# The spiking network's first product as one float32 product, without high and low halves

## What is computed

```
x = x + layernorm(L0_ffn(layernorm(x)))
# L0_ffn(x, W_fc, W_proj):
h = square(relu(einsum('bsd,fd->bsf', x, W_fc)))     # 128 -> 512: the first product
y = einsum('bsf,df->bsd', h, W_proj)                 # 512 -> 128
# five steps; spikes are counted:
reset = spike(mem - 1); mem = 0.9 * mem + y - reset; spk = spike(mem - 1)
return sum(spks) / 5
```

## Time and profile before

| | us |
|---|---|
| median of 3 runs | 934.92 |
| lowest, highest | 934.91, 935.84 |
| profiled execution, its own time | 935.99 |
| its span (first to last instruction) | 934.1 |
| TensorE busy | 818.9 (88%) |
| VectorE busy | 682.9 (73%) |
| ScalarE busy | 586.2 (63%) |
| GpSimd busy | 430.6 (46%) |
| TensorE granted clock, mean | 0.954 of 2.4 GHz |

### The profile page before, as it was taken

The page is one execution under the profiler, slowest core; times in us unless marked ns, Lnnn a source line. Parts: engine busy times, 40 slices in busy tenths (PEclk is TensorE's granted clock), DMA queues, the critical chain, the costliest instruction groups (busy, mean ns, idle before and its releaser), DMA issues. The chain is left out here.

```text
span 934.1 us, 15863 instructions
## 1 busy us (share of the span) xinstructions
PE 818.9 (88%) x5364; PEld 713.6 (76%) x5364; DVE 682.9 (73%) x1919; ACT 586.2 (63%) x1244; POOL 430.6 (46%) x737
## 2 busy tenths in 40 slices
PE   0789889999999999999999999998959888877664
PEld 0688778888888888888888888987748676765553
DVE  4667878887888888878888878676448876677741
ACT  2545657777777777777777777675665456443343
POOL 6653424544454445444544454334444433344333
PEclk9969989999999999999999999999979899999986
DMA  9100000000001000100010000000000000000001
GB/s 292 27 1 2 1 1 1 13 23 1 1 2 35 1 1 2 35 1 2 1 35 2 1 1 1 2 1 1 2 1 1 1 1 1 12 12 12 11 12 34
DMA packets 19726, 13.68 MB, mean 15 GB/s; under 512 B 2487, under 2 KB 18494, under 8 KB 19646
## 3 DMA queue, kind: packets, MB, share of 16 engines
q1 hardware_dynamic: 18924, 12.47, 4.6%
q10 hardware_dynamic: 722, 0.20, 0.1%
HBM read 10.57 MB, written 2.10 MB: 14 GB/s over the span
## 5 line engine op out<-in xcount | busy, mean ns | idle before, releaser
L311 PE MATMUL PS<-W,HL 128*128 128x128 f32 x1536 | 202.6, 276 | 0.0
L311 PEld LDWEIGHTS PS<-W,HL 128*128 128x128 f32 x1536 | 194.2, 192 | 8.1
L696 POOL TENSOR_TENSOR JOIN<-STATS 128x8 f32<-128x8 f32 (+1 forms) x58 | 15.5, 267 | 238.0 <-DVE STATS L1136 238.0
L873 ACT ACTIVATE HL<-PS 128x512 f32<-128x512 f32 x192 | 109.3, 594 | 19.3 <-PE PS L311 15.0
L943 ACT ACTIVATE EK<-PS,NKM 128x512 f32<-128x512 f32 x48 | 33.0, 688 | 99.6 <-DVE NKM L1246 99.6
L311 PE MATMUL PS<-X2H,W1L 128*128 128x512 f32 x192 | 88.9, 463 | 6.1 <-issue 3.8
L859 ACT ACTIVATE XR<-XI,RSTD 128x128 f32<-128x128 f32 x224 | 71.7, 396 | 33.2 <-POOL RSTD L713 30.0
L1136 DVE BATCH_NORM_STATS2 STATS<-XI 128x6 f32<-128x128 f32 x416 | 89.4, 278 | 1.8 <-POOL JOIN L697 1.5
L752 POOL TENSOR_TENSOR QB<-QB,QRC 128x512 f32<-128x512 f32 x48 | 50.9, 1060 | 81.0 <-DVE QRC L1277 81.0
L321 PE MATMUL PS<-ID,XR 128*128 128x128 f32 x416 | 65.6, 281 | 21.8 <-ACT XR L859 21.7
L321 PEld LDWEIGHTS PS<-ID,XR 128*128 128x128 f32 x416 | 48.7, 143 | 37.9 <-issue 18.8
(11 more groups left out here) (207 smaller groups left out, 2133.4 us busy)
## 6 DMA issues: line engine op xcount, KB each, us to landing
W<-in_w SPq DMA_DIRECT2D x12, 256.0 KB
X<-in_x SPq DMA_DIRECT2D x8, 256.0 KB, 5.0
out<-X SPq DMA_DIRECT2D x8, 256.0 KB, 2.3
QKV<-in_qkv SPq DMA_DIRECT2D x6, 192.0 KB, 3.3
FWD<-in_fwd SPq DMA_DIRECT2D x1, 1024.0 KB, 6.1
INV<-in_inv SPq DMA_DIRECT2D x1, 1024.0 KB, 8.8
WO<-in_wo SPq DMA_DIRECT2D x6, 64.0 KB
FWDX<-in_fwdx SPq DMA_DIRECT2D x1, 256.0 KB, 6.4
```

What stands on the lines that cost most here:

```text
L311: return nc.tensor.matmul(o, l, r, start=start, stop=stop, skip_group_check=True)
L873: nc.scalar.activation(HL[f][:, :], pH[f % 2][:, :], ACT.Prelu, alpha=LEAK).then_inc(s["hl"], 1)
```

## The change

The spiking network's first product becomes one float32 product, FCC x X2F, in place of three. ScalarE writes twice the centred weights once, as float32 (FCC), and signals fc_out itself; VectorE's FCL goes. ScalarE copies the transposed input of items 48 to 55 into X2F (float32) and not into X2H; X2L is made for items 0 to 47 alone. h 0, state_turn and shift_turn wait for ScalarE's copy (x2h) where they waited for X2L. ScalarE's copy gets two waits, since X2F is now read by TensorE and, for the last item of the layers, by VectorE.

```
-        FCH, FCL = sb("FCH", [FB * P], F32R), sb("FCL", [FB * P], F32R)
+        FCC = sb("FCC", [FB * P])
...
                 if f == 0:
                     if item < ITEMS:
                         pe.wait_ge(s["w1_lo"], item // BATCH + 1)
+                        pe.wait_ge(s["x2l"], item + 1)
                     else:
                         pe.wait_ge(s["fc_out"], 1)
-                    pe.wait_ge(s["x2l"], item + 1)
+                        pe.wait_ge(s["x2h"], item + 1)
...
-                high, low = (W1H[w], W1L[w]) if item < ITEMS else (FCH, FCL)
                 o = slice(f * P, (f + 1) * P)
-                split3(pH[f % 2][:, :], high[:, o], low[:, o], X2H[:, :], X2L[:, :]).then_inc(s["h_ps"], 1)
+                if item < ITEMS:
+                    last = split3(pH[f % 2][:, :], W1H[w][:, o], W1L[w][:, o], X2H[:, :], X2L[:, :])
+                else:
+                    last = mm(pH[f % 2][:, :], FCC[:, o], X2F[:, :])
+                last.then_inc(s["h_ps"], 1)
...
             def state_turn(v, n):
                 pe.wait_ge(s["st_x"], v + 1)
-                pe.wait_ge(s["x2l"], min(n - 1, ALL))
+                pe.wait_ge(s["x2h"], min(n - 1, ALL))
...
-                    copy(X2H[:, :], pX2[:, :]).then_inc(s["x2h"], 1)
+                    if n - 2 == ITEMS:
+                        act.wait_ge(s["x2l"], ITEMS)
+                    act.wait_ge(s["h_ps"], (n - 2) * FB)
+                    copy(X2F[:, :], pX2[:, :]).then_inc(s["x2h"], 1)
...
-                    nc.scalar.activation(FCH[:, :], pW[:, :], ACT.Copy, scale=2.0).then_inc(s["fc_hi"], 1)
+                    nc.scalar.activation(FCC[:, :], pW[:, :], ACT.Copy, scale=2.0).then_inc(s["fc_out"], 1)
...
-                full = X2F if n - 2 < ITEMS else pX2
-                tt(X2L[:, :], full[:, :], X2H[:, :].bitcast(FP32), ALU.subtract).then_inc(s["x2l"], 1)
+                tt(X2L[:, :], X2F[:, :], X2H[:, :].bitcast(FP32), ALU.subtract).then_inc(s["x2l"], 1)
...
-                    dve.wait_ge(s["fc_hi"], 1)
-                    stt(out=FCL[:, :], in0=pW[:, :], scalar=2.0, in1=FCH[:, :].bitcast(FP32), op0=ALU.mult,
-                        op1=ALU.subtract).then_inc(s["fc_out"], 1)
...
-                if has_x:
+                if 2 <= n < ITEMS + 2:
                     second_low(n)
...
-                if has_x:
-                    second_low(n)
```

More of the change, by code:

```diff
@@ L232, in build @@
             "bias_out bias_ps bm_out bm_ps bo_c bo_mean bo_st c_in c_ps cdb ce1 ce1_zero ct e1 e1_arg e2 e2_arg eighth "
-            "ek ekT_ps ek_tm fc_hi fc_out fc_ps g_ps gt h_ps hl i_rstd i_st i_var i_ve k_fm k_out k_ps k_rec k_skip "
+            "ek ekT_ps ek_tm fc_out fc_ps g_ps gt h_ps hl i_rstd i_st i_var i_ve k_fm k_out k_ps k_rec k_skip "
             "kf kf_ps kmax ktm la la_exp late_in ln1_half ln1_rstd ln2_rstd ln_part m_ps m_ready mbv mixed out_ps p_const "
@@ L1201, in late_weights @@
             def late_weights(n):
-                if n == CENTRE:
-                    dve.wait_ge(s["fc_hi"], 1)
-                    stt(out=FCL[:, :], in0=pW[:, :], scalar=2.0, in1=FCH[:, :].bitcast(FP32), op0=ALU.mult,
-                        op1=ALU.subtract).then_inc(s["fc_out"], 1)
                 if n == CENTRE_IN:
```

## The result

| | before | after |
|---|---|---|
| median of 20 runs, us | 935.23 | 939.65 |
| lowest, highest, us | 931.95, 941.68 | 935.46, 941.61 |
| profiled execution, its own time, us | 935.99 | 939.09 |
| its span, us | 934.1 | 937.1 |
| mean granted clock | 0.954 | 0.954 |

What follows compares the result with a forecast made beforehand. TensorE was taken as nearly full in the layers, and each late step as a ring through several engines. Losses of 1.44 us less 0.3 gave +1.1 us, so 936.1 us, range 933.5 to 938.6.

Steps and rivals of the forecast that it cites:

- The price of a product: Late steps' h products: one plain product costs 0.08 us more than three passes at full clock, bounds 0 and 0.16.
- its own sign: Late stretch changing by over 2 us with the same clock in the steps: a product's price or the cover is wrong.
- Its other sign: A step's granted clock has changed, which the busy time by stretch shows: the prediction is wrong by a clock rival.
- What is on the path: Late steps: h 2, h 3 and the first item's h 0 count, thirteen full-clock terms, 1.04 us, 0.88 after hidden ones.
- The centring step: Where the weights are centred, at 569: without FCL the h product starts sooner, a gain of 0.3 us (0 to 0.54).
- X2L at nothing: Late steps: eight subtractions of 0.69 us each leave VectorE, 5.5 us in all, costed at nothing.
- Rival C: X2L was on the path: seven items give back 0.28 to 0.69 us each; 933.9 to 931.0 us, chance 0.05.
- Products at the low clock: Four items begin their step at the low clock: 0.28 us each, 1.12 together, of which half, 0.56, was taken.
- Rival A: Moved pauses lose a step's clock, perhaps at 763.85: 1.3 to 2.95 us on top, 937.4 to 939.1, chance 0.24.
- Rival B: Longer h 0 and h 1 shorten pauses and keep the clock at 739.10 or 791.00: 2.6 us each, 933.5, chance 0.12.
- Rival D: The single instruction runs in three reduced passes' time, term 0; only the 0.3 gain is left: 934.6 us, chance 0.07.
- the ring: Late steps: ScalarE, TensorE, then VectorE and GpSimd in turn; TensorE stands still 3.41 to 5.78 us before h 2.

Runs made afterwards that it cites:

- the doubled products: The changed kernel with h 2 and h 3 of the spiking network each computed twice, 16 products more: 950.88 us, ratio to before 1.0156.
- the filled pair: Before and after, both with the second, larger set of unread products of constants in TensorE's pauses: 926.38 and 927.65 us.
- experiment 4: The changed kernel with sixteen products computed twice: h 2 and h 3, 950.88 us; or h 0 and h 1, 935.60 us.
- experiment 5: The changed kernel with three unread products of constants in one pause, the one at 765.53: 937.36 us, ratio to before 1.0003.
- the wide plan of fillers: Unread products of constants in TensorE's pauses, more than in a first set; in the kernel before: 926.38 us, ratio 0.9876.

## Why the prediction was right in its range and low in its sum

- **The price of a product: the step that failed.** The sum took 0.08 us, from the product's first start to the next start. The traces show 0.16 to 0.17. For h 3 the 0.86 us of the product itself was right (0.87 measured; "WK times SH" was the right row, and the doubled products confirm it), but the product also starts 0.08 us later behind the y ahead of it (0.89 against 0.81 us). For h 2, behind a pause, the product itself is dearer by 0.16 (0.96 against 0.80). The interval to measure was from the start of the instruction ahead, or from the end of the pause, to the start of the one behind; the 0.16 that I had as upper bound was the value. The Trainium skill (FP8 and Floating Point Precision, section TensorE Precision Notes) has true FP32 as four passes, an estimated 0.92 us at the earlier trace rows's 0.23 (the prediction wrote 0.93); the doubled products measured 0.86, so its direction (dearer than three passes) holds and the estimate is 0.06 high here. With 0.16 for 0.08 the sum would have been 11 x 0.16 + 0.56 - 0.3 = 2.0 us. By its own sign (over 2 us in the late stretch at the same clock) the prediction had the price wrong: the filled pair shows 2.35. Its other sign, a step's granted clock that has changed, came as well.
- **What is on the path: right.** h 2 and h 3 cost, h 0 and h 1 don't but for the first item's (+0.18). The two products of the step at 716.83 are hidden by the transform's wait for back_bands, as predicted. Those of the step behind it (739.10) are hidden in the same way when the clock is full; before, that step ran partly at the low clock and had no such wait. At full clock this adds up: 0.18 for the first h 0, eight times 0.33, less two times 0.35 and the 0.10 behind the seventh step, is 2.0 us, and with the 0.35 of the wait behind the last item 2.4.
- **The centring step: right.** 0.3 was predicted, 0.32 measured, and FCL alone does it.
- **X2L at nothing: nearly right.** Rival C (0.28 to 0.69 us an item given back) falls, at full clock and in one trace a kernel: with X2L kept, the seven steps take the same 115.53 us. But the relief is not even nothing: once, behind the last item, it costs 0.35 us, which nothing in the prediction allowed for.
- **Products at the low clock.** I gave four of them 0.28 us and halved it. Measured at the low clock, h 2 of the third step takes 1.44 us before and 1.87 after (684.63 to the y at 686.50): 0.43 more and not 0.28, since h 2's own price is 0.16 and not 0.08 at full clock. What is left of that when the clock rises, no run isolates from the question of where the low clock falls.
- **Rival A came on top.** At full clock the change costs 2.35 us in the late part and gives 0.32 back in the centring step: 2.0 us. That the corrected sum above is 2.0 as well is in part chance: it holds 0.56 for products at the low clock, which the filled pair doesn't have, and nothing for the wait behind the last item. In the unfilled executions that were profiled it is 3.57 in the late part, and the 1.2 between is where the low clock fell: +1.30 in the third step, +0.55 in the fourth, -1.53 in the sixth, +1.91 in the seventh, each against the filled pair's difference, and -0.98 behind them. The step at 763.85, "so near the edge that a later start of 0.2 to 0.4 us may lose it", did lose its clock, though it came 1.7 us later, not 0.2 to 0.4. How systematic the clock's part is, the medians don't settle: the ratio's interval is 2.0 to 4.9 us, and 2.0 is what full clock leaves. So 2.0 of the 3.4 us is shown, and 1.4 is open. That the range held is partly luck: its upper part was drawn for the loss of one step's clock, and what came was the net of losses and gains in five places, on top of a price twice that of the sum.
- **Rival B**: the mechanism is shown by experiment 4 for products of 0.86 us more. In the change itself the pauses before h 2 became 0.16 to 0.33 us shorter, as rival B said, and the two steps that it named took less: from h 2 to h 3 7.59 us for 8.91, and 6.20 at full clock for 8.56. This gain of after sits beside rival A's loss. But the shorter pause isn't shown to be its cause: in the same execution a pause of the same 3.25 us lost the clock at 765.53, and in experiment 5 the step at 742.02, with after's code, took 1.45 us more. **Rival D** falls with the price of FCC's products.

Of the forms that compute all that the reference asks and ran more than once, the kernel before with the wide plan of fillers is the fastest: 926.38 us, 1.24% (0.97 to 1.51%) below before. The same fillers in after give 0.92% (0.68 to 1.15%), and with X2L kept 925.45 us in a single run; these don't stand apart.

## What to carry to other kernels

Price a product that replaces others from the start of the instruction ahead to the start of the one behind, on both kernels: an instruction's own extent misses by how much the next one starts later behind its predecessor. Price it at each kind of place: behind a pause the difference was 0.16 us in the product itself. Fewer instructions, or the 4.3 us of subtractions taken off VectorE in seven steps, are worth nothing where the ring runs through another engine. And where pauses lie at the edge of what keeps the clock, separate the two parts before judging an edit: fill the pauses in both kernels and compare the difference there.

## What the runs showed of the hardware that I had not expected

- Work that nobody needs can pay. Fillers in the pauses took 1.24% off the time of before; 16 doubled products in front of the pauses brought the ratio to before from 1.0036 to 0.9985. The Trainium skill (TensorE: Matmul & The Clock Gate, section Why this matters for your kernels) warns of idle gaps between bursts; these runs agree in kind. A gap's length alone doesn't decide here: 3.25 us before 765.53 was followed by the low clock, and 3.25 us before 794.57 in the same execution by the full one:

```profile
794.57 1.13 PE L311 MATMUL PS<-X2F,FCC 128*128 128x512 f32 x2 [3.25 <-ACT HL L882]
```

- The low clock can begin inside a pause and be spent there. Two executions with mean clocks 0.78 and 0.80 over the same step differed by 1.64 us, of which 0.34 is the products' price, because the low part lay more in the pause in one and on the work in the other. So the mean granted clock of a stretch doesn't price it; its busy part does.
- Executions of one kernel differ in it: after ran from 935.46 us (mean clock 0.957) to 941.61 (0.945), though not in strict order (938.08 us at 0.948, 939.09 at 0.954).
- With eight subtractions taken off VectorE it waited longer: 3.56 us for 3.21 before the same addition, undone by one instruction that nobody reads.
